# Edge-matrix build of a four-layer graph network: two wide VectorE instructions per batch in place of five, four GpSimd copies in place of one, counts evicted apart from weights

## The reference, cut to what matters

```python
msg = (h * norm_src)[src]
agg = jax.ops.segment_sum(msg, dst, num_segments=N_NODES)     # layer 0, ten times
msg = h[src] * norm[:, None]                                  # layer 1; norm holds edge_weight
out = jax.ops.segment_sum(msg, dst, num_segments=n)
```

## Time and profile before

| | us |
|---|---|
| median of 3 runs | 3188.61 |
| lowest, highest run | 3164.35, 3189.68 |
| the profiled execution | 3168.94 |
| its span in the trace | 3167.1 |
| granted TensorE clock over the span | 0.938 of full speed |
| busy over the span: PE, DVE, ACT, POOL | 2711.2, 2309.3, 1604.7, 1515.5 |

### The profile page before, as it was taken

How to read it: one execution, slowest core, us unless ns; L and a number is a source line. 1 busy time by engine, 2 the same in 40 slices (tenths; PEclk the granted TensorE clock), 3 DMA queues, 4 the chain that set the end, 5 groups by cost and what they waited for, 6 DMA issues and landing times. The chain is left out here.

```text
span 3167.1 us, 69319 instructions
## 1 busy us (share of the span) xinstructions
PE 2711.2 (86%) x18402; PEld 1813.6 (57%) x18402; DVE 2309.3 (73%) x6740; ACT 1604.7 (51%) x4593; POOL 1515.5 (48%) x1524
## 2 busy tenths in 40 slices
PE   2777777789989899778898888898887999999998
PEld 1566665344444444357777777777764555555556
DVE  5999998587786412677777777777887777777772
ACT  1688888033332000145555555555564666666666
POOL 2122211044442100267777777777306777777770
PEclk7999999899999899799999999999887999999995
DMA  1122222166664955443433333333104544444440
GB/s 38 74 89 89 89 89 95 38 228 221 217 225 151 387 234 233 164 115 81 86 82 81 81 84 82 80 82 82 48 15 108 130 130 126 132 131 125 130 113 12
DMA packets 438165, 379.89 MB, mean 120 GB/s; under 512 B 164968, under 2 KB 375896, under 8 KB 437832
## 3 DMA queue, kind: packets, MB, share of 16 engines
q1 hardware_dynamic: 396104, 330.85, 33.4%
q0 software_dynamic: 41584, 44.48, 6.9%
q10 hardware_dynamic: 144, 0.41, 0.0%
HBM read 287.22 MB, written 88.32 MB: 119 GB/s over the span
## 5 line engine op out<-in xcount | busy, mean ns | idle before, releaser
L1434 POOL DMA_INDIRECT big<-row_table,src x710 | 676.0, 952 | 231.1 <-issue 166.7
L2188 POOL DMA_INDIRECT big<-message_table,src x542 | 535.6, 988 | 230.7 <-issue 157.4
L2227 PE MATMUL banks<-big 128*128 128x512 f16 x1650 | 422.6, 380 | 9.0 <-DVE big L2302 9.0
L2320 DVE TENSOR_SCALAR big<-big 128x2048 f16<-128x2048 f16 (+2 forms) x396 | 422.4, 1067 | 1.4 <-DMA big<-shifted_keys 1.1
L512 PE MATMUL banks<-work 128*128 128x226 f16 x1197 | 312.4, 261 | 105.2 <-ACT banks L543 46.5
L931 PE MATMUL banks<-big,work 128*128 128x512 f16 (+1 forms) x1750 | 361.5, 366 | 16.7 <-PEq L702 16.7
L1847 DVE TENSOR_REDUCE big<-banks 128x1 f32<-128x256 f32 x451 | 190.5, 422 | 172.5 <-PE banks L1751 159.9
L1751 PE MATMUL banks<-big 97*128 x902 | 301.5, 417 | 1.9 <-DMA big<-q_table 1.9
L513 PE MATMUL banks<-work 128*128 128x200 f16 x1197 | 300.6, 251 | 0.0
L514 PE MATMUL banks<-work 128*128 128x200 f16 x1197 | 298.6, 249 | 0.0
L931 PEld LDWEIGHTS banks<-big,work 128*128 128x128 f16 x1750 | 161.3, 102 | 196.9 <-issue 43.4
(11 more groups left out here) (409 smaller groups left out, 6190.8 us busy)
## 6 DMA issues: line engine op xcount, KB each, us to landing
big<-weights_halves SPq DMA_DIRECT2D x12, 6400.0 KB, 23.9
big<-shifted_keys SPq DMA_DIRECT2D x66, 640.0 KB
weights_dense<-work SPq DMA_DIRECT2D x196, 200.0 KB, 1.9
weights_halves<-work SPq DMA_DIRECT2D x98, 400.0 KB, 2.7
work<-weights_dense SPq DMA_DIRECT2D x74, 400.0 KB, 4.2
big<-q_table SPq DMA_DIRECT2D x451, 64.0 KB
big<-in_ef SPq DMA_DIRECT2D x403, 64.0 KB
big<-in_ea SPq DMA_DIRECT2D x403, 32.0 KB
```

Of the source, the lines that this page charges most:

```text
L1434: po.indirect_dma_start(rows[:, t % RT, s, 0:D], None, x_t.rearrange("a p c -> (a p) c"), bass.IndirectOffsetOnAxis(ap=m.src2[:, s, t:t + ...
L2188: po.indirect_dma_start(G[n % R][:, s, :], None, g_t.rearrange("a p c -> (a p) c"), bass.IndirectOffsetOnAxis(ap=m.src2[:, s, t:t + 1], ax ...
L2227: pe.matmul(psH[q % 2], table[:, a, :, :].rearrange("p s d -> p (s d)"), hot[:, 2 * TE * a:2 * TE * (a + 1)], start=(a == 0), stop=(a == N ...
L2320: dve.tensor_scalar(hot[:, 2 * TE * a:2 * TE * (a + n)], key[q % 2][:, 0:n, :], place[:, BATCHES.index((a, n)):BATCHES.index((a, n)) + 1], ...
```

## The change

All one-hots of a batch come from one comparison. The row one-hot (128), the column one-hot (200) and the chunk one-hot (26) are laid in one run of 364 numbers per visit (`HOTS`), cut in 14 pieces of 26 (5 for the row, 8 for the column, 1 for the chunk), and each piece has its key pair; the column and chunk keys are raised by 130 and 338 (`COL_AT`, `CHUNK_AT_HOT`). The numbers 0 to 363 are written once in f16 by an added cast in `stage_tables`. The two products of the weights become one instruction of 2560 elements. POOL writes the 14 key pairs of a visit with three copies (100, 160 and 20 elements per batch) and the weight pairs with a fourth (40 elements). The wait for the one-hots now stands directly behind the instruction that makes them. PE's first matmul takes its stationary operand out of the run of 364 and has 234 columns (226 before). On ACT the weights (400) and the counts (400) leave PSUM in two instructions, the counts straight to `big`; the third instruction from `pairs` is gone, `pairs` has half its size, and the zeroing waits for both.

```diff
-                po.tensor_copy(twice[b % 2], m.tabs5()[:, :, b * TP:(b + 1) * TP].unsqueeze(3).to_broadcast([P, 5, TP, 2])).then_inc(doubled, 1)
+                hots, weights = twice[b % 2]
+                tab = lambda i: m.tab(i)[:, b * TP:(b + 1) * TP]
+                at = 0
+                for i, n in ((ROW, ROW_PIECES), (COL, COL_PIECES), (CHUNK, 1)):
+                    po.tensor_copy(hots[:, :, at:at + n, :].rearrange("p t k u -> p t (k u)"), tab(i).unsqueeze(2).to_broadcast([P, TP, 2 * n])).then_inc(doubled, 1)
+                    at += n
+                po.tensor_copy(weights, m.tabs5()[:, WHI:WLO + 1, b * TP:(b + 1) * TP].unsqueeze(3).to_broadcast([P, 2, TP, 2])).then_inc(doubled, 1)
...
-                dve.wait_ge(doubled, b + 1)
-                dve.tensor_tensor(pairwise(rows[:, 0, :, :]), iota(P), value(ROW, P), ALU.is_equal).then_inc(rows_ready, 1)
-                dve.tensor_tensor(pairwise(cols[:, :, 0:CW]), iota(CW), value(COL, CW), ALU.is_equal)
-                dve.tensor_tensor(pairwise(cols[:, :, CW:CAW]), iota(CAW - CW), value(CHUNK, CAW - CW), ALU.is_equal)
+                dve.wait_ge(doubled, b * 4 + 4)
+                dve.tensor_tensor(cols, iota, hots, ALU.is_equal).then_inc(rows_ready, 1)
                 dve.wait_ge(rows_ready, b + 1)
-                for i, kind in ((1, WHI), (2, WLO)):
-                    ins = dve.tensor_tensor(pairwise(rows[:, i, :, :]), pairwise(rows[:, 0, :, :]), value(kind, P), ALU.mult)
-                ins.then_inc(oh_ready, 1)
+                once = cols[:, :, 0:P].unsqueeze(1).to_broadcast([P, 2, TP, P])
+                dve.tensor_tensor(rows, once, weights, ALU.mult).then_inc(oh_ready, 1)
...
-                    pe.matmul(to(CW, CW + CAW), rows[:, 0, t, :], cols[:, t, :], start=False, stop=True, skip_group_check=True)
+                    pe.matmul(to(CW, CW + CAW), cols[:, t, 0:P], cols[:, t, COL_AT:HOTS], start=False, stop=True, skip_group_check=True)
...
-                    act.wait_ge(cast, q - 1)
-                nc.scalar.activation(pairs[i % 2].rearrange("p ka (b w) -> p ka b w", b=2), sums[i], ACT.Copy, scale=WDOWN).then_inc(evicted, 1)
+                nc.scalar.activation(pairs[i % 2].rearrange("p a (b w) -> p a b w", b=2), sums[i][0], ACT.Copy, scale=WDOWN).then_inc(evicted, 1)
+                nc.scalar.copy(to.rearrange("p a (b w) -> p a b w", b=2), sums[i][1]).then_inc(cast, 1)
                 if not first or q:
                     act.wait_ge(evicted, q)
+                    act.wait_ge(cast, q)
                     at = 2 * ((i - 1) % 4)
                     nc.scalar.copy(m.PS[:, at:at + 2, 0:2 * CW], zero.unsqueeze(2).to_broadcast([P, 2, 2 * CW])).then_inc(freed, 1)
-                act.wait_ge(evicted, q + 1)
-                nc.scalar.activation(to, pairs[i % 2][:, NCH:2 * NCH, :], ACT.Copy, scale=1.0 / WDOWN).then_inc(cast, 1)
```

More of the change, by code:

```diff
@@ L53 @@
 CW = NCH * BB
-CAW = CW + NCH + 1
+PIECE = NCH + 1
+ROW_PIECES, COL_PIECES = -(-P // PIECE), -(-CW // PIECE)
+PIECES = ROW_PIECES + COL_PIECES + 1
+HOTS = PIECES * PIECE
+COL_AT, CHUNK_AT_HOT = ROW_PIECES * PIECE, (PIECES - 1) * PIECE
+CAW = HOTS - COL_AT
+DEGREE_AT = CW + CHUNK_AT_HOT - COL_AT
 BANKS = 8
@@ L319, in _ @@
             chain(dve.tensor_copy(m.iotaH[:, :], iotaI[:, 0:CW]))
+            chain(dve.tensor_copy(m.hot_numbers(), iotaI[:, 0:HOTS]))
             dve.wait_ge(s_last, 32)
@@ L430, in stage_build @@
             h16 = home.bitcast(F16)
[L431 to L435, removed]
+            rows = h16[:, 0:2 * TP * P].rearrange("p (i t r) -> p i t r", i=2, t=TP)
+            slots.append((rows, h16[:, 2 * TP * P:].rearrange("p (t c) -> p t c", t=TP)))
+        pairs = [m.work2[:, size + i * BCOL:size + (i + 1) * BCOL].rearrange("p (a w) -> p a w", w=2 * BB) for i in range(2)]
+        twice = []
+        for i in range(2):
+            at = size + 2 * BCOL + i * TP * (PIECES + 2)
+            of_slot = m.work2[:, at:at + TP * (PIECES + 2)].bitcast(F16)
+            twice.append((of_slot[:, 0:2 * TP * PIECES].rearrange("p (t k u) -> p t k u", t=TP, k=PIECES),
+                          of_slot[:, 2 * TP * PIECES:].rearrange("p (k t u) -> p k t u", k=2, t=TP)))
         zero = m.colsN[:, 0, 0:1]
@@ L460, in _ @@
             dve.memset(zero, 0.0).then_inc(init, 1)
-            iota = lambda n: m.iotaH[:, 0:n].rearrange("p (r u) -> p r u", u=2).unsqueeze(1).to_broadcast([P, TP, n // 2, 2])
-            pairwise = lambda a: a.rearrange("p t (r u) -> p t r u", u=2)
+            iota = m.hot_numbers().unsqueeze(1).to_broadcast([P, TP, HOTS])
             def batch(b, k, first=False):
                 rows, cols = slots[k]
-                value = lambda i, n: twice[k][:, i, :, :].unsqueeze(2).to_broadcast([P, TP, n // 2, 2])
+                hots, weights = twice[k]
+                hots = hots.rearrange("p t k u -> p (t k) u").unsqueeze(2).to_broadcast([P, TP * PIECES, PIECE // 2, 2])
+                weights = weights.rearrange("p k t u -> p (k t) u").unsqueeze(2).to_broadcast([P, 2 * TP, P // 2, 2])
                 if not first:
@@ L490, in _ @@
             chain = m.dve_step.on(dve)
[L491 removed]
+            chain(dve.tensor_copy(dout, m.PS[:, 0, DEGREE_AT:DEGREE_AT + NCH]))
             for b in range(1, BANKS):
[L493 removed]
+                chain(dve.tensor_tensor(dout, dout, m.PS[:, b, DEGREE_AT:DEGREE_AT + NCH], ALU.add))
         @block.tensor
@@ L511, in batch @@
                     to = lambda c0, c1: flat[:, bass.ds(places[t] + c0, c1 - c0)]
-                    pe.matmul(to(CW, CW + CAW), rows[:, 0, t, :], cols[:, t, :], start=False, stop=True, skip_group_check=True)
-                    pe.matmul(to(0, CW), rows[:, 1, t, :], cols[:, t, 0:CW], start=False, stop=True, skip_group_check=True)
-                    pe.matmul(to(0, CW), rows[:, 2, t, :], cols[:, t, 0:CW], start=False, stop=True, skip_group_check=True).then_inc(vis_done, 1)
+                    col = cols[:, t, COL_AT:COL_AT + CW]
+                    pe.matmul(to(CW, CW + CAW), cols[:, t, 0:P], cols[:, t, COL_AT:HOTS], start=False, stop=True, skip_group_check=True)
+                    pe.matmul(to(0, CW), rows[:, 0, t, :], col, start=False, stop=True, skip_group_check=True)
+                    pe.matmul(to(0, CW), rows[:, 1, t, :], col, start=False, stop=True, skip_group_check=True).then_inc(vis_done, 1)
             pe.wait_ge(init, 1)
@@ L528, in _ @@
             act.wait_ge(init, 1)
-            sums = [m.PS[:, 2 * i:2 * i + 2, 0:2 * CW].rearrange("p b (ka w) -> p ka b w", w=BB) for i in range(BANKS // 2)]
+            sums = [[m.PS[:, 2 * i:2 * i + 2, k * CW:(k + 1) * CW].rearrange("p b (a w) -> p a b w", w=BB) for k in range(2)] for i in range(BANKS // 2)]
             def evict(q, i, end, to):
```

10 lines of the change are left out of this document (6 added, 4 removed).

## The result

The changed kernel takes 3175.72 us (median of 20 runs, 3170.78 to 3209.77), the kernel before 3163.32 us (median of 20 runs, 3157.99 to 3189.68). The ratio is 1.0046, with a 95% interval of 1.0027 to 1.0065: 8.5 to 20.6 us slower. Of the 20 runs of the kernel before, 17 lie between 3157.99 and 3169.76 us and three between 3183.41 and 3189.68, and two of these three (3188.61 and 3189.68, 25 and 26 us above the median of the 20) were among the three shown ahead of the prediction.

What follows compares the result with a forecast made beforehand. PE's register load was taken to bound the stage, with POOL's four copies then making DVE's batch 3.90 us: leg 7.90 against 7.60, +18 us on 3188.61, giving 3207 us; own range 3194 to 3217, whole range 3174 to 3248.

Steps and rivals of the forecast that it cites:

- Which engine sets the stage: Stage 86 to 546 us: PE with its 2.00 us register load, floor 7.40 us a leg, rising to 7.47; not DVE.
- The rates of the new instructions: DVE's batch: comparison of 3640 elements 2.05 us, product of 2560 elements 1.48 us, 0.04 us between them.
- Rival 4: DVE's comparison leaves the fast rate because its inputs differ in shape: batch +1.9 us, some +225 us; chance 0.03.
- The lock and the order of the copies: POOL against DVE's port lock: first copy ahead of the comparison, second in the middle, two behind the product, tail 0.25 us.
- Rivals 1 and 3: 1: copies hidden, PE keeps the stage, -8 to +4 us, chance 0.15; 3: all four copies trail, +60 us, chance 0.08.
- rival 2: First copy misses the comparison's start, so three copies trail the product: tail 0.51 us, leg 8.16, +33 us; chance 0.25.
- The size: Whole run: leg 7.90 against 7.60 us, +0.30 x 59.5 = +18 us, the rest netting to nothing.
- The batch: DVE's batch with POOL's copies: 0.06 + 2.05 + 0.04 + 0.02 + 1.48 + 0.25 = 3.90 us, leg 7.80.
- The allowance of 0.10 us a leg for disturbances by PE: Half of the distance between mean leg and floor kept, raising the leg from 7.80 to 7.90 us.
- Start and end: Added cast about 0.4 us and first batch's wait +0.5 us, cancelled by -0.9 us from ACT's evictions at the end.
- a tail of 0.40 us: Upper end of the forecast's own range, copies behind the product: tail 0.15 to 0.40 us, said to give +5 to +28 us.
- The level: Forecast time of the run: median of the runs 3188.61 + 18 = 3207 us; from the profiled execution, 3187.

Runs made afterwards that it cites:

- wider_load: Kernel before, with the one load of a leg fetching 28 registers instead of 24, four unused: leg 8.30 us, ratio 1.0110 (1.0062 to 1.0159).
- late_first: Changed kernel with a POOL memset of 128 f32 elements ahead of each batch's four copies: leg 8.18 us, ratio 1.0109 (1.0077 to 1.0141) to the kernel before.
- one_product_gv10: Kernel before with both products in one instruction and 22 registers loaded a leg instead of 24: ratio 1.0569 (1.0543 to 1.0596).
- gv10: Kernel before with PE waiting for free banks every tenth visit, not every fifth, so 22 registers a leg: leg 10.57 us, ratio 1.0578 (1.0549 to 1.0607).

## Why the prediction was right or wrong

**Which engine sets the stage: right.** PE's standstill ahead of a leg is the register load (1.85 us of the 2.00), it grows with the registers, and the leg grows with it: in wider_load, where the clock stayed up, to 7.66 with a floor of 20 x 0.27 + 2.23 = 7.63. The rest of the growth to 7.92 and 8.30 was the clock, which the prediction didn't have. With POOL out of the way the leg fell to 7.50, near the floor of 7.47, not to DVE's 2 x 3.57. No kernel reached 1% below the kernel before. A faster DVE, a faster ACT and earlier banks gave -0.05, +0.04 and 0.00 us more, the second mostly by one drop of the clock.

**The rates of the new instructions: right.** Comparison 2.05 us by itself, product 1.49, 0.03 to 0.04 us between them. Rival 4 (the fast rate lost) did not happen.

**The lock and the order of the copies: right.** First copy ahead of the comparison, second in the middle, third through with the product, fourth alone behind it; 0.25 us of idle time, the sum that was forecast, though its parts are 0.21 for the fourth copy and 0.04 to DVE's start, where the prediction had 0.07, 0.16 and 0.02. Rivals 1 and 3 did not happen; rival 2 is what late_first brings about in every batch, and it happened in 7 of 115 batches of the changed kernel. The Trainium skill, "VectorE: DVE Perf Modes", section "The DRAIN you can't avoid", has a semaphore between VectorE instructions cost nothing extra, measured there on a chain of copies. The 0.035 us between comparison and product, where instructions without a wait overlap by 0.08, don't agree.

**The size: too high, by three terms.** Forecast +18 us; the profiled stage gives +8.4, the medians of 20 runs differ by 12.4.
- The batch was put at 3.90 us and takes 3.85. The first copy holds the comparison by 0.03 (2.08 against 2.05), not 0.06, and the second holds the product by nothing that can be seen (0.035 us between them, not 0.06). Over 119 batches this is 5 to 6 us.
- The allowance of 0.10 us a leg for disturbances by PE was a choice, half of what lay between mean and floor before. It turned out 0.04 (7.75 against 2 x 3.855 = 7.71): when POOL sets the pace, PE's own unevenness is absorbed. That is 3 to 4 us. The 0.04 holds the seven batches of rival 2's order as well.
- Start and end were put at nothing together and give -0.7 us.

The forecast's own range has a slip: by the same sum a tail of 0.40 us gives +36 us, not +28 (+30 without the 0.10 for disturbances). This slip didn't move the forecast itself.

**The level: wrong, and this is the larger error.** The forecast of 3207 us was the change added to a median of three runs, 3188.61. Twenty runs have their median at 3163.32. The profiled execution of the kernel before, 3168.94 us, lay between, and the text chose to carry its distance of 19.67 us to the median over to the result. So the step that failed is the last one, "Against the median of the runs, 19.67 us higher, it is 3188.61 + 18": of the 31 us between 3207 and the measured 3175.72, 25 are this base (3188.61 against 3163.32) and 6 the size of the change (18 against 12.4). That 3175.72 still lies in the stated 3174 to 3248 is luck: this range starts so low because of the scatter of the runs, and the forecast's own range, 3194 to 3217, missed. Against 3163.32 the forecast reads +1.4%, the ratio of the runs is +0.46%. With only three runs, which lie 25 us apart, the profiled execution's own time, 3168.94 + 18 = 3187, was the better base, and the change itself should have been what is forecast.

**What stays open.** The ratio's interval is 8.5 to 20.6 us; the stage as profiled explains 8.4. The rest of the program lasts 2608 to 2620 us behind the end of the stage in the profiles, whatever was edited (2619.8 before, 2619.0 changed, 2610.5 in the repeat of the kernel before); only in one_product_gv10, whose profiled execution lies 26 us above the median of its runs, is it 2638.9. A few microseconds more than the stage's can hide in that, and no run separates them.

## What to carry to other kernels

Ask of an engine that shares a port with a busy one not how long its instructions are but how many openings the other leaves: here each GpSimd copy needs a boundary between VectorE instructions, and fusing VectorE's five instructions into two took the boundaries away just when the copies were quadrupled. Fuse on the one side only if the other side fuses as well; a deeper buffer doesn't mend a rate. And state a forecast as a difference to a profiled execution, not as a level on a median of three.

## What the runs showed of the hardware that was not expected

- GpSimd copies that stand ready while VectorE works with two SBUF inputs get through where VectorE really waits between its instructions: the opening of 0.035 us between comparison and product let a copy through every time. Before the change 8 of some 57 missed every opening where the instructions overlapped. At the comparison's start it is a race: 0.09 us ahead a copy of 100 elements ran in 0.27 us and cost the comparison 0.03, 0.06 to 0.14 us behind it waited 2.03 to 2.12.
- A GpSimd memset of 128 f32 elements, which only writes, started 0.09 us ahead of a VectorE instruction with two SBUF inputs, took 0.20 us and cost it 0.01 (2.06 against 2.05). What a memset that starts behind it would do wasn't run.
- A load of registers from SBUF for PE takes about 0.06 us a register: 0.33 us for 4, 1.36 for 20, 1.61 for 24, 1.86 for 28, at the least. With 22 a leg every second load took 5.43 to 5.78 us (gv10). The page of the profile names such a wait "issue" or another engine; the durations are found by the load's source line.
- TensorE's granted clock fell with small additions to the gap. With a median gap of 1.97 us ahead of each leg it is 1.00 from 120 us on, in the changed kernel too; with 2.10 and 2.23 us it is 0.95 and 0.92 from 86 to 540 us, and single stretches run at the lower level of 1.2 GHz (0.40 us for a matmul that takes 0.27). A leg with such a stretch took about 8.5 us in place of 7.6, and the leg behind it 8.0 to 8.4.
